# Turning a tile's rows by VectorE in 32x32 blocks instead of by TensorE, with four block loads a tile and the result stores issued by ScalarE

## The reference

```
x = x + tanh(g_xattn) * xattn(layernorm(x), ctx, ctx)      # 8 heads over the token axis
y = layernorm(x)                                           # 2048 x 512
probs = softmax(y @ w_router)                              # 2048 x 16
topk_w, topk_ids = top_k(probs, 4); topk_w /= sum(topk_w)
g = y @ w_gate[e];  u = y @ w_up[e]                        # 512 x 256 for each of 16 experts
moe_out = sum over the token's 4 experts of  topk_w * ((silu(g) * u) @ w_down[e])
shared  = (silu(y @ w_sh_gate) * (y @ w_sh_up)) @ w_sh_down  # inner width 1408
out = x + tanh(g_ffn) * (moe_out + sigmoid(y @ w_sh_expert_gate) * shared)
```

## Time and profile before

| | us |
|---|---|
| median of three runs | 1233.71 |
| profiled execution, its time | 1237.59 |
| profiled execution, its span | 1235.9 |
| PE busy (share of the span) | 1166.2 (94%) |
| DVE busy | 728.2 (59%) |
| ACT busy | 522.4 (42%) |
| POOL busy | 607.0 (49%) |
| routed experts, first to last `up` matmul start | 710.2 to 1088.6 |
| landing of a load of a tile's rows, min / median / max | 2.5 / 2.7 / 6.1 |
| landing of a store of results, min / median / max | 2.0 / 2.1 / 6.1 |

### The profile page before, as it was taken

The page is one execution under the profiler, slowest core; times in us unless marked ns, Lnnn a source line. Parts: engine busy times, 40 slices in busy tenths (PEclk is TensorE's granted clock), DMA queues, the critical chain, the costliest instruction groups (busy, mean ns, idle before and its releaser), DMA issues.

```text
span 1235.9 us, 21535 instructions
## 1 busy us (share of the span) xinstructions
PE 1166.2 (94%) x6020; PEld 786.1 (64%) x6021; DVE 728.2 (59%) x1083; ACT 522.4 (42%) x1056; POOL 607.0 (49%) x603
## 2 busy tenths in 40 slices
PE   1899999999999979999699999999999999999996
PEld 0344444444444348877488778887888888888885
DVE  5789888888888318754043533333333333337877
ACT  1588887887778811111011133333333333321110
POOL 3245645554553243156627156465654654327753
PEclk9999999999999989999799999999999999999998
DMA  9476667666764139853723245546455464423655
GB/s 241 118 185 193 199 189 196 187 198 189 195 190 129 53 111 407 290 198 107 257 85 142 80 142 166 199 164 203 162 170 202 162 202 164 152 90 95 175 170 187
DMA packets 104815, 214.58 MB, mean 174 GB/s; under 512 B 12352, under 2 KB 17472, under 8 KB 104768
## 3 DMA queue, kind: packets, MB, share of 16 engines
q1 hardware_dynamic: 85408, 152.08, 40.0%
q0 software_dynamic: 18016, 61.88, 15.3%
q10 hardware_dynamic: 1344, 0.04, 0.1%
HBM read 117.48 MB, written 91.75 MB: 169 GB/s over the span
## 4 chain that ended last, share of the span: by engine, by line
PE 61%; issue 1%; DVE 1%; DVEq 0%; ACT 0%
PE score_ps L135 19%; PE score_ps L1558 18%; PE d_ps L1508 10%; PE d_ps L1582 9%; PE score_ps L1534 3%; PE d_ps L1572 1%; PE d_ps L1461 1%; DVE y_all L1355 1%; DVE y_all L1343 0%; DVEq L158 0%; PE d_ps L1484 0%; PE score_ps L1470 0%; DVE hid L1425 0%; PE d_ps L1477 0%; DVE th L1420 0%
## 5 line engine op out<-in xcount | busy, mean ns | idle before, releaser
L662 DVE TENSOR_REDUCE maxima<-score_ps 128x2 f32<-128x1024 f32 x256 | 301.4, 1218 | 44.2 <-PE score_ps L754 40.2
L609 ACT ACTIVATE probs<-sb_ps 128x512 f32<-128x512 f32 x512 | 266.2, 596 | 50.7 <-PE sb_ps L781 49.4
L135 PE MATMUL score_ps<-yn_t,w_split 128*128 128x512 f32 x1056 | 257.7, 402 | 10.6 <-issue 7.4
L1558 PE MATMUL score_ps<-w_split,x_split 128*128 x948 | 254.0, 405 | 0.0
L135 PEld LDWEIGHTS score_ps<-yn_t,w_split 128*128 128x128 f32 x1056 | 201.2, 191 | 63.4 <-issue 11.7
L1072 POOL CAST w_split<-w_raw 128x1024 fp32r<-128x1024 f32 x63 | 65.9, 1046 | 246.4 <-POOLq L1142 120.7
L1558 PEld LDWEIGHTS score_ps<-w_split,x_split 128*128 128x128 f32 x948 | 166.5, 189 | 26.3
L1074 POOL TENSOR_TENSOR w_split<-w_raw,w_split 128x1024 fp32r<-128x1024 f32 x63 | 151.9, 2411 | 5.2
L792 PE MATMUL o_ps<-probs,v_t 128*17 128x512 f32 x1024 | 136.5, 605 | 0.7 <-ACT o_sb L575 0.7
L1508 PE MATMUL d_ps<-w_split,h_split 128*128 128x512 f32 x528 | 127.5, 395 | 6.0 <-issue 5.9
L1582 PE MATMUL d_ps<-w_split,h_rows 128*128 x474 | 122.5, 394 | 1.1 <-issue 0.9
(11 more groups left out here) (149 smaller groups left out, 1362.7 us busy)
## 6 DMA issues: line engine op xcount, KB each, us to landing
xs_dram<-zero SPq DMA_DIRECT2D x1, 20224.0 KB, 58.6
stage<-xs_dram SPq DMA_DIRECT2D x79, 256.0 KB, 2.7
res_dram<-stage SPq DMA_DIRECT2D x79, 256.0 KB, 2.1
k_dram<-k_hi SPq DMA_DIRECT2D x16, 512.0 KB, 2.8
q_dram<-q_hi SPq DMA_DIRECT2D x16, 512.0 KB, 2.8
w_raw<-in_L_ffn_w_gate_dram POOLq DMA_DIRECT2D x16, 512.0 KB
w_raw<-in_L_ffn_w_up_dram POOLq DMA_DIRECT2D x16, 512.0 KB
w_raw<-in_L_ffn_w_down_dram POOLq DMA_DIRECT2D x16, 512.0 KB
```

The lines of the kernel that those rows point to most:

```text
L135: mm = pe.matmul(dst[i], w[:, k, f * P:(f + 1) * P], self.yn_t[:, b, k, t * self.SPAN:(t + 1) * self.SPAN], start=(n == 0), stop=(n == 3 * ...
L609: act.activation(probs[:, c % 2, head(j)[2], :], sb_ps[:, bank_of_score(HG * c + j), :], ACT.Exp, scale=SCALE).then_inc(exp_done, 1)
L662: dve.tensor_reduce(maxima[q % 2][:, :].rearrange("p (h u) -> p u h", u=8)[:, u, :], sa_ps[:, pair_of_unit(q, g, u), :, :], AX_X, ALU.max) ...
L1558: mm = pe.matmul(gu_ps[j], x_split[j][:, b, k, :], w_split[:, bass.ds(at + (a * 3 * ex.PIECE + k * 2 * FE), 2 * FE)], start=(n == 0), stop ...
```

## The change

The rows of a tile are loaded as blocks, so that a transposition within 32x32 blocks turns the whole tile. Four DMAs, q = 0 to 3, each bring the features 128q to 128q+127 of all 128 rows into partitions 32q to 32q+31: row 32b+i, feature 128q+y go to partition 32q+i, place 128b+y. Each run in memory is 128 elements, 512 bytes, instead of a row of 2048. One DVE instruction (`turn_rows`, STREAM_TRANSPOSE) then writes to the same PSUM bank as before, so that partition p holds the features 4p to 4p+3. The contraction is in another order than before, so `load_expert` reads the gate and up weights of an expert with rows 4p to 4p+3 in partition p as well. `upper_rows` and `lower_rows` read the bank through a view that puts blocks side by side. `store_rows` leaves SP's list for ACT's, behind the upper hidden of the tile, and `upper_rows` moves behind it; on DVE `lower_rows` moves behind the lower hidden.

```diff
     def load_expert(self, eng, e, landed):
         both = self.w_raw[:, 0:2 * self.PIECE].rearrange("p (k c) -> p k c", k=self.KC)
         for i in range(2):
             eng.dma_start(both[:, :, i * self.FE:(i + 1) * self.FE],
-                          self.we[i][e].rearrange("(k p) f -> p k f", p=P)).then_inc(landed, 16)
+                          self.we[i][e].rearrange("(p k) f -> p k f", p=P)).then_inc(landed, 16)
...
+    def turned_rows(j):
+        return xt_ps[j].rearrange("p (b c i) -> p c b i", b=4, c=KC)
+
+    def split_rows(j, a):
+        return x_split[j][:, a, :, :].rearrange("p c (b i) -> p c b i", b=4)
...
         def load_rows(i, j):
-            sp.dma_start(x_rows[j][:, :], xs_dram[bass.ds(i * P, P), :]).then_inc(x_loaded[j], 16)
-
-        def store_rows(i, j):
-            sp.wait_ge(res_done, i + 1)
-            sp.dma_start(res_dram[bass.ds(i * P, P), :], res[j][:, :]).then_inc(res_stored[j], 16)
+            for q in range(4):
+                sp.dma_start(x_rows[j][32 * q:32 * q + 32, :].rearrange("i (b y) -> i b y", b=4),
+                             xs_dram[bass.ds(i * P, P), q * P:(q + 1) * P].rearrange("(b i) y -> i b y", b=4)).then_inc(x_loaded[j], 16)
 
         def tile(i, j):
             if not isinstance(i, int) or i + 3 < NTILE:
                 sp.wait_ge(xt_done, i + 2)
                 load_rows(i + 3, 1 - j)
-            if not (isinstance(i, int) and i == 0):
-                store_rows(i - 1, 1 - j)
...
     def _(act):
...
-            act.activation(x_split[j][:, 0, :, :].rearrange("p k t -> p (k t)"), xt_ps[j], ACT.Copy).then_inc(xhi_done, 1)
+            act.activation(split_rows(j, 0), turned_rows(j), ACT.Copy).then_inc(xhi_done, 1)
...
+        def store_rows(i, j):
+            act.wait_ge(res_done, i + 1)
+            act.dma_start(res_dram[bass.ds(i * P, P), :], res[j][:, :]).then_inc(res_stored[j], 16)
...
                 result(i - 1, 1 - j)
-            if ahead(i):
-                upper_rows(i + 2, j)
             act.wait_ge(ht_done, i + 1)
...
             act.activation(h_rows[j][:, 0, :, :].rearrange("p f t -> p (f t)"), ht_ps[j], ACT.Copy).then_inc(hthi_done, 1)
+            if not (isinstance(i, int) and i == 0):
+                store_rows(i - 1, 1 - j)
+            if ahead(i):
+                upper_rows(i + 2, j)
...
     def _(dve):
...
+        def turn_rows(i, j):
+            if first_two(i):
+                dve.wait_ge(hid_done, TILES_A)
+            dve.wait_ge(x_loaded[j], 64 * (i // 2) + 64 if isinstance(i, int) else 64 * pair[0] + 128)
+            if not first_two(i):
+                dve.wait_ge(xlo_done, i - 1)
+            dve.transpose(xt_ps[j].rearrange("p (b c i) -> p b c i", b=4, c=KC),
+                          x_rows[j][:, :].rearrange("p (b i c) -> p b c i", b=4, c=KC)).then_inc(xt_done, 1)
+
         def lower_rows(i, j):
             dve.wait_ge(xhi_done, i + 1)
-            dve.tensor_tensor(x_split[j][:, 1, :, :].rearrange("p k t -> p (k t)"), xt_ps[j],
-                              x_split[j][:, 0, :, :].rearrange("p k t -> p (k t)").bitcast(F32), ALU.subtract).then_inc(xlo_done, 1)
+            dve.tensor_tensor(split_rows(j, 1), turned_rows(j), split_rows(j, 0).bitcast(F32), ALU.subtract).then_inc(xlo_done, 1)
...
             if ahead(i):
-                lower_rows(i + 2, j)
+                turn_rows(i + 2, j)
             dve.wait_ge(hthi_done, i + 1)
...
                               h_rows[j][:, 0, :, :].rearrange("p f t -> p (f t)").bitcast(F32), ALU.subtract).then_inc(htlo_done, 1)
+            if ahead(i):
+                lower_rows(i + 2, j)
...
         for i in range(2):
+            turn_rows(i, i)
+        for i in range(2):
             lower_rows(i, i)
...
     def _(pe):
...
-        def turn_rows(i, j):
-            pe.wait_ge(x_loaded[j], 16 * (i // 2) + 16 if isinstance(i, int) else 16 * pair[0] + 32)
...
-            for k in range(KC):
-                mm = pe.transpose(xt_ps[j][:, k * P:(k + 1) * P], x_rows[j][:, k * P:(k + 1) * P], ident[:, :])
-            mm.then_inc(xt_done, 1)
...
         def tile(i, j, at, following):
...
-            if ahead(i):
-                turn_rows(i + 2, j)
```

More of the change, by code:

```diff
@@ L1220, in _ @@
         result(NTILE - 1, (NTILE - 1) % 2)
+        store_rows(NTILE - 1, (NTILE - 1) % 2)
         act.wait_ge(ehid_done, NTILE)
@@ L1411, in chunk @@
                         add_rows(b, c.unit(t))
+        def turn_rows(i, j):
[6 more added lines that the diff above has]
+                          x_rows[j][:, :].rearrange("p (b i c) -> p b c i", b=4, c=KC)).then_inc(xt_done, 1)
         def lower_rows(i, j):
             dve.wait_ge(xhi_done, i + 1)
-            dve.tensor_tensor(x_split[j][:, 1, :, :].rearrange("p k t -> p (k t)"), xt_ps[j],
-                              x_split[j][:, 0, :, :].rearrange("p k t -> p (k t)").bitcast(F32), ALU.subtract).then_inc(xlo_done, 1)
+            dve.tensor_tensor(split_rows(j, 1), turned_rows(j), split_rows(j, 0).bitcast(F32), ALU.subtract).then_inc(xlo_done, 1)
+        pair = [None]
         def tile(i, j):
@@ L1435, in _ @@
         for i in range(2):
+            turn_rows(i, i)
+        for i in range(2):
             lower_rows(i, i)
         accumulate(early[-1], NT - 1)
-        tiles_in_turn(dve, tile)
+        for i in range(2):
+            tile(i, i)
+        with dve.Fori(1, (NTILE - 3) // 2) as r:
+            for j in range(2):
+                pair[0] = r
+                tile(2 * r + j, j)
+        for i in range(NTILE - 3, NTILE):
+            tile(i, i % 2)
         for n, c in enumerate(late):
@@ L1525, in chunk @@
                     down(before, NT - 1)
-        def turn_rows(i, j):
-            pe.wait_ge(x_loaded[j], 16 * (i // 2) + 16 if isinstance(i, int) else 16 * pair[0] + 32)
-            if first_two(i):
-                pe.wait_ge(hid_done, TILES_A)
-            else:
-                pe.wait_ge(xlo_done, i - 1)
-            for k in range(KC):
-                mm = pe.transpose(xt_ps[j][:, k * P:(k + 1) * P], x_rows[j][:, k * P:(k + 1) * P], ident[:, :])
-            mm.then_inc(xt_done, 1)
         def kept_values():
@@ L1552, in up @@
             pe.wait_ge(xlo_done, i + 1)
-            if not first_two(i):
+            if first_two(i):
+                pe.wait_ge(hid_done, TILES_A)
+            else:
                 pe.wait_ge(ehid_done, i - 1)
@@ L1585, in down_rows @@
             mm.then_inc(tile_done, 1)
-        pair = [None]
         kept = [pe.alloc_register(f"kept{n}") for n in range(3)]
@@ L1609, in _ @@
             chunk(c, early[n - 1] if n else None)
-        for i in range(2):
-            turn_rows(i, i)
         down(early[-1], NT - 1)
@@ L1625, in _ @@
             for j in range(2):
-                pair[0] = r
                 at, following = tile(2 * r + j, j, at, following)
```

1 line of the change is left out of this document (removed).

## The result

| | before | changed |
|---|---|---|
| median of four runs, us | 1234.27 (1232.26 to 1235.61) | 1218.43 (1218.07 to 1221.37) |
| profiled execution, its span, us | 1235.9 | 1216.3 |
| PE busy, us | 1166.2 | 1137.3 |
| DVE busy, us | 728.2 | 813.3 |

The ratio is 0.988, with a 95% interval of 0.9863 to 0.9897: 15.8 us faster, where 35 were forecast. The direction is right and the upper end of the range, 1219, just reaches the time; the size is not right, less than half of what was forecast, and the rest of this document is about the missing 19 us.

The account below looks back on a forecast made before the run. PE was taken to bound the experts' stage: 34.7 us from 77 tiles plus 0.8 for the first two, 35.5 off 1237.6, all else 0; 1198.2 against the median, plus 1 for waits: 1199 us, range 1191 to 1219.

Parts of the forecast that it names:

- PE sets the pace in this stage: Experts' steady part: PE, busy 372.9 of 374 us, sets the pace; waits of ACT and DVE are slack.
- An instruction off PE's list is worth 0.45 us: PE's list: four products fewer a tile save 4.78 less 4.33 us, 34.7 us over 77 tiles.
- The kernel before contains the case itself: Last tiles of the kernel before, with nothing left to turn, were taken to show the new period, 4.33 us.
- The transposition: DVE's new instruction: 0.69 us, range 0.49 to 1.94, in DVE's idle time; PE waits only from 2.1 us.
- The store on ACT: ACT's list: issue of some 0.6 us, ahead of the upper rows; PE waits only from 1.0 us; cost 0.
- Loading in four: SP's list: four DMAs for one, 1.4 to 1.7 us a tile, landing within the 8.0 us available; cost 0.
- The weights' order at zero: Experts' weight loads: same bytes, longer reads in memory, cost 0.
- The rival of late DMAs: Weight and row loads become late and delay the kernel by 8 to 18 us, to 1207 to 1217; 20%.
- first half: POOL's weight loads: slack of 2 us a cycle shrinks to 0.3, so delays of 1 or 2 us cost time.
- The issue that is dear on ACT itself: Rival: the store's issue takes 1.1 to 1.3 us, PE waits, 8 to 23 us back, 1207 to 1222; 8%.
- the slow transposition: Rival: DVE becomes the bound, slower kernel from 2.4 us a transposition; at 2.9 us, 36 us more, 1270; 8%.
- Something else in the stage, PE's own list included, fills the 0.45 us again: Rival of no change: the time saved a tile in the experts' stage is used up again; 4%.

Follow-up runs that it names:

- e4: The kernel before, turn of the rows still on PE, with one table read moved ahead of the hidden turn: 1211.90 us, ratio 0.9966 to the kernel before.
- e1: The changed kernel with one of PE's two table reads a tile moved ahead of the wait for the hidden rows: 1182.36 us, ratio 0.9741 to the kernel before.
- f2: e1 run a second time, as base for other variants: 1184.05 us, ratio 0.9748 to the kernel before.
- e6: The changed kernel with the transposition reading 32 adjacent elements instead of every fourth: 1201.33 us, ratio 0.9876 to the kernel before.
- e7: The changed kernel with one load of 128 whole rows a tile instead of four loads of blocks: 1196.78 us, ratio 0.9845 to the kernel before.
- e8: The changed kernel with the stores of results issued by SP again instead of ACT: 1193.91 us, ratio 0.9821 to the kernel before.
- f3: f2 with the experts' gate and up weights read in the old order of rows: 1181.95 us, ratio 0.9731 to the kernel before.
- e3: The changed kernel with a third table read a tile, its value unused, behind the other two: 1229.91 us, ratio 1.0116 to the kernel before.

## Why the prediction was off

*PE sets the pace in this stage: half right.* The array was busy for 372.9 of 374 us, and the rest of the path, PE's own sequencer included, was taken to have time. An array that is never idle does not say how far ahead of it its sequencer is. It was hardly ahead: the 11 short waits of the kernel before say so, and e4, in which they go and 4.7 us with them.

*An instruction off PE's list is worth 0.45 us: the failed step.* "The kernel before contains the case itself" was the reasoning: a tile without L1534 takes 4.33 us. But that tile differs from the others in two things. `ahead(i)` is false for it, and `ahead(i)` guards the turn of the rows **and** `weights_of(i + 2)`. It lacks the two table reads too, 0.77 us and more each, and so it could not show that they would come to the end of the queue. With the turn alone removed the late tile takes 4.85 us and the other 4.45, 4.67 on average, 0.19 us less than before instead of 0.45. So the term that was put at 77 x 0.45 = 34.7 us measured 15.1: the sequencer's way from the hidden rows to the down matmuls, 3.2 us where 2.67 were to be had, was put at nothing.

With one read out of the way as well, e1 and f2 are 34 and 32 us below the kernel before, near the 35 forecast; but 4.7 us of this the early read brings in the kernel before too (e4). With the read moved in both kernels the change is worth 29.5 us: a tile goes from 4.77 to 4.33 us, 76 x 0.44 = 33.4, and 4 us of it are lost, mostly in the seven long tiles of e1, for which the forecast had put 1 us.

*The transposition: right in its effect, 1.11 us instead of 0.69.* It runs in DVE's idle time, as said, and at neighbouring elements the same instruction takes 0.72 (e6), with the same time for the kernel. The estimate of 1.04 from the strided reduction was the better one to choose. The Trainium skill's one element per cycle per lane (Vector Engine (DVE) Microarchitecture Reference, section 3.8) fits e6's 0.72 us, since other operations of DVE with 512 elements a lane take 0.69; its remark on reads that step over 16-byte lines (SBUF — State Buffer, "Door 1: The DMA port swizzle") fits the 0.39 us between the two. Both hold here, each for its own access.

*The store on ACT: cheaper than said on ACT, and dear in a place nobody looked.* 0.34 us for the issue, and it runs while ACT still copies the upper hidden: the upper rows begin 905.92 - 905.64 = 0.28 us after it, not 0.6. DVE's lower rows end at 907.24, half a microsecond ahead of the next product at 907.75. But 7.6 us of the kernel's time hang on it, through PE's second table read.

*Loading in four: right beside SP, wrong at zero.* SP has time for it, 0.32 us each, and the loads land in 2.3 us; DVE waited for one in three of the 79 tiles, 2.3 us in all. The 4.7 us of e7 come, by the sum under e8, through the read again.

*The weights' order at zero:* right, f3 shows no difference.

*The rival of late DMAs.* Its first half came true without its price. With 4.42 us a tile POOL waits for its weights' DMA 12 times (e1), so it has become as slow as its DMAs, as computed; but the split is still through in time, and at most the 4 us of e1's long tiles can be its doing. The issue that is dear on ACT itself, and the slow transposition, were not the case. *"Something else in the stage, PE's own list included, fills the 0.45 us again"* got 4%. It was this one, by half.

## What to carry to other kernels

An engine that is busy for 99.7% has two halves, the queue's issue and the array, and only one of them is seen in the busy share: before a product is taken off, add up what the sequencer must do between the last wait that it passes and the next matmul (register operations, table reads) and hold it against the work queued on the array. Here that was 3.2 us against 2.67. A tile that seems to contain the case is a measure only if everything that its guard switches off is known. Reads of tables by a busy engine belong ahead of its waits, one at a time with matmuls between them; that was worth 17 to 19 us here, more than the change itself.

## What was not expected of the hardware

- A read of one word of SBUF into a register of PE takes 0.30 us, and with its register operations 0.77 us from start to start. Two in a row use up what nine matmuls of 512 columns (some 2.1 us on the array) leave over.
- The same read takes 0.71 us (up to 1.19) in one place of the list and only in the first of the two turns of the loop's body, 0.61 with fewer DMA issues by SP and 0.48 with none by ACT, and 0.30 where it stands apart from the other (e1, e4). In the kernel before it took 0.52 us in the even tiles and 0.56 in the odd ones (medians), and under a tile of 4.78 us that hardly showed. The cause is open.
- A shortage of the sequencer need not show in every turn: here it was in the even tiles alone, and of a third read of 0.77 us in each tile (59 us in 77 tiles) only 28 were felt (e3).
- A transposition of 128x512 float32 elements in 32x32 blocks by DVE takes 1.11 us where the reads step 16 bytes and 0.72 where they are neighbours.
